# Unit-matrix products in the first cross-attention's last tiles and in TensorE's pauses at the heads and ends of the stages

## What is computed

```python
x = x + L0_xattn(ln(x), ctx, ctx, ...)      # 16 heads of 8, keys: 77 context tokens
x = x + L0_ffn(ln(x), ...)                  # 8 experts, relu, top 2, hidden 512
x = x + L1_xattn(ctx, ln(x), ...)           # latent attention: 16 heads of 64, keys: 77 context tokens and the 512 latents
x = x + L1_ffn(ln(x), ...)                  # 8 experts, swiglu, sampled number of experts
x = x + L2_xattn(ctx, ctx, ln(x), mask)     # 16 heads of 8, additive mask
x = x + L2_ffn(ln(x), ...)                  # mixture of 12, gelu, routed twice
x = x + L3_xattn(ln(x), ctx, mask)          # 8 heads of 64
x = x + L3_ffn(ln(x), ...)                  # 1 shared and 8 routed experts, gelu
```

```python
h = act(einsum('nd,df->nf', normed, W1[e]) + b1[e])
y = y + cw[:, e:e+1] * (h @ W2[e] + b2[e])
```

## Time and profile before

| | |
|---|---|
| median of 3 runs | 1892.74 us (1891.47 to 1894.18) |
| the profiled execution's own time | 1898.05 us |
| its span | 1896.2 us |
| TensorE busy | 1769.7 us (93%), weight loads 1304.8 us (69%) |
| VectorE, ScalarE, POOL busy | 77%, 55%, 37% |
| mean granted clock of TensorE | 0.966 |
| chain that ended last, by engine | PE 5%, DVE 1% of the span |

### The profile page before, as it was taken

The page is one execution under the profiler, slowest core; times in us unless marked ns, Lnnn a source line. Parts: engine busy times, 40 slices in busy tenths (PEclk is TensorE's granted clock), DMA queues, the critical chain, the costliest instruction groups (busy, mean ns, idle before and its releaser), DMA issues. The chain is left out here.

```text
span 1896.2 us, 29215 instructions
## 1 busy us (share of the span) xinstructions
PE 1769.7 (93%) x10747; PEld 1304.8 (69%) x10747; DVE 1461.0 (77%) x2712; ACT 1037.0 (55%) x1570; POOL 707.2 (37%) x571
## 2 busy tenths in 40 slices
PE   5998999779999999999989999799899999989898
PEld 4767888555655655655557777677658889957676
DVE  6877997767677777777767888799799955667798
ACT  3656888557777777777654555355200310055685
POOL 3632322145556556556430444455112301012131
PEclk9988999889999999999988999899899999999899
DMA  2001221100000000000001211000000010000032
GB/s 68 2 7 50 83 68 56 53 1 1 1 1 1 1 1 1 1 1 1 1 20 57 67 67 56 13 2 1 18 22 22 28 56 1 0 13 2 30 112 100
DMA packets 21191, 51.46 MB, mean 27 GB/s; under 512 B 3563, under 2 KB 11383, under 8 KB 18116
## 3 DMA queue, kind: packets, MB, share of 16 engines
q1 hardware_dynamic: 20596, 49.53, 7.7%
q10 hardware_dynamic: 464, 0.20, 0.1%
HBM read 48.48 MB, written 1.25 MB: 26 GB/s over the span
## 5 line engine op out<-in xcount | busy, mean ns | idle before, releaser
L1615 POOL TENSOR_TENSOR sb_L_total<-sb_L_total,sb_L_probT 128x512 f32<-128x512 f32 x128 | 161.4, 1293 | 170.4 <-ACT sb_L_probT L1953 170.4
L441 POOL TENSOR_TENSOR sb_L_prob<-sb_L_prob,sb_L_rsum 128x616 f32<-128x616 f32 (+1 forms) x96 | 105.7, 1123 | 227.9 <-DVE sb_L_rsum L743 227.9
L2021 DVE TENSOR_REDUCE sb_L_tops<-banks 128x2 f32<-128x1024 f32 x128 | 156.4, 1223 | 23.8 <-PE banks L1729 22.5
L1953 ACT ACTIVATE sb_L_probT<-banks 128x1024 f32<-128x1024 f32 x128 | 124.8, 1025 | 74.5 <-PE banks L1763 74.0
L1776 PE MATMUL banks<-sb_L_probT,sb_L_v 128*64 128x512 f32 x512 | 129.0, 605 | 0.0
L2403 DVE SCALAR_TENSOR_TENSOR sb_L2f_hid<-banks,sb_L2f_weight,sb_L2f_hid 128x512 f32<-128x512 f32 x176 | 122.0, 744 | 3.0 <-PE banks L97 1.6
L1612 POOL TENSOR_TENSOR sb_L_total<-sb_L_probT 128x512 f32<-128x512 f32 x64 | 93.7, 1488 | 78.9 <-ACT sb_L_probT L1953 78.9
L2473 DVE SCALAR_TENSOR_TENSOR sb_resid<-banks,sb_L2f_weight,sb_resid 128x128 f32<-128x128 f32 x192 | 67.1, 351 | 62.5 <-PE banks L97 57.9
L1315 DVE TENSOR_TENSOR sb_L0f_hid_low<-sb_L0f_raw,sb_L0f_hid_high 128x1024 fp32r<-128x1024 f32 x64 | 88.5, 1398 | 31.9 <-ACT sb_L0f_hid_high L1271 31.6
L1252 ACT ACTIVATE sb_L1f_gate<-banks 112x512 f32<-112x512 f32 x96 | 57.5, 599 | 91.3 <-PE banks L97 90.8
L529 PE MATMUL banks<-sb_ident,sb_L_prob 128*77 128x128 f32 x640 | 97.9, 286 | 5.7 <-POOL sb_L_prob L441 5.4
(11 more groups left out here) (433 smaller groups left out, 5336.0 us busy)
## 6 DMA issues: line engine op xcount, KB each, us to landing
sb_L0f_wide<-spread_L0f SPq DMA_DIRECT2D x7, 1024.0 KB, 6.9
sb_L1f_wide<-spread_L1f SPq DMA_DIRECT2D x7, 1024.0 KB, 7.7
sb_L3f_wide<-spread_L3f SPq DMA_DIRECT2D x7, 1024.0 KB, 4.7
sb_fetched<-L2f_w SPq DMA_DIRECT2D x12, 256.0 KB, 2.6
sb_fetched<-L1f_gu SPq DMA_DIRECT2D x8, 336.0 KB, 3.3
sb_fetched<-L0f_w SPq DMA_DIRECT2D x8, 259.0 KB, 2.8
sb_fetched<-L0f_w SPq DMA_DIRECT2D x8, 256.0 KB, 3.2
sb_normT<-L2f_w SPq DMA_DIRECT2D x2, 768.0 KB, 4.1
```

Source lines behind the costliest of these rows:

```text
L441: pool.tensor_tensor(grid, grid, bcast(rsum[:, n % PROBS, half], [None, KEYS]), ALU.mult).then_inc(normed, 1)
L1615: pool.tensor_tensor(sums, sums, probT[:, k, h], ALU.add).then_inc(added[h], 1)
L1953: act.activation(probT[:, k], ps[:, slot:slot + 2, :], ACT.Exp).then_inc(exped, 1)
L2021: dve.tensor_reduce(tops[:, :, k, 0], ps[:, banks:banks + 2, :], AX.X, ALU.max).then_inc(bound_read, 1)
```

## The change

It adds `keep_busy` in seven places of the code, and ahead of two of them a wait. In the order of the program: 8 products ahead of the key projection of each cross-attention (three stages); 5 in each of L0's last three tiles, before the third group's product, behind a wait that the scores of tile 15 have been read (`wait_scores_read`), because bank 0 held them; after the router's matmuls 20 in L0f and 6 in L3f; 10 at the end of L0f and L1f, ahead of the turn of the next norm; in latent attention 12 ahead of the first projection, 4 between two sums of squares, and 8 ahead of the turn of the maxima, behind a wait that VectorE has read the fourth bound, which stood further down before.

```diff
--- before.py
+++ after.py
@@ -467,6 +467,7 @@
             @block.tensor
             def _(pe):
                 fetch.wait(pe, "w")
+                keep_busy(pe, c, 3 if split else 2, 8)
                 for j in range(FB):
                     pe.matmul(ps[:, K_AT[j], 0:BATCH * KEYS], wk[:, j * P:(j + 1) * P], c.ctxT[:].rearrange("p b k -> p (b k)"),
                               start=True, stop=True).then_inc(k_done, 1)
@@ -572,6 +573,9 @@
                             turn(n, g + 1)
                         if g == SCORES_AT and later(n, AHEAD):
                             scores(n + AHEAD)
+                        elif g == SCORES_AT and split and not on_pe:
+                            wait_scores_read(TILES - 1)
+                            keep_busy(pe, c, 0, 5)
                         product(n, g)
                         next_queries()
                     if SCORES_AT == GROUPS and later(n, AHEAD):
@@ -1216,6 +1220,8 @@
                         hidden(s, f)
                 norm.wait(pe)
                 route.tensor(pe)
+                if not gated:
+                    keep_busy(pe, c, YBANKS[0], 20 if folded else 6)
                 norm.wait_parts(pe)
                 for s in range(STEPS):
                     then = s + lag
@@ -1233,6 +1239,7 @@
                         turn_back(s - STEPS + BATCH - 1)
                 if nxt is not None:
                     pe.wait_ge(out_read, STEPS - 1)
+                    keep_busy(pe, c, YBANKS[(STEPS - 3) % len(YBANKS)], 10)
                     nxt.norm.turn(pe, 0, SIDE)
                     nxt.norm.turn(pe, 1, YBANKS[(STEPS - 2) % len(YBANKS)])
                 turn_back(BATCH - 1)
@@ -1778,6 +1785,7 @@
                             last = pe.matmul(O[HEAD[h]], vc[:, p % 2, b, HEAD[h]], probT[0:KEYS, k, h, :], start=False, stop=True)
                     last.then_inc(pv_done, 1)
 
+                keep_busy(pe, c, 0, 12)
                 use_side(KC, 0)
                 fetch.wait(pe, "values")
                 use_side(VC, 0)
@@ -1787,6 +1795,7 @@
                 use_side(NKC, 0)
                 use_side(NKL, 0)
                 wait_read(pe, KC, 0)
+                keep_busy(pe, c, 0, 4)
                 use_side(NQL, 0)
                 norm.wait_parts(pe, 1)
                 wait_read(pe, VC, 0)
@@ -1814,6 +1823,8 @@
                 bound(0, 3, 0)
                 bound(0, 4)
                 wait_read(pe, Q, 1)
+                pe.wait_ge(bound_read, 4)
+                keep_busy(pe, c, 0, 8)
                 use_side(MT, 0)
                 wait_read(pe, V4, 0)
                 wait_read(pe, NQL, 1)
```

## The result

The changed kernel takes **1905.39 us** (median of 6 runs, 1903.11 to 1909.06), the kernel before 1893.53 beside it (1891.47 to 1894.62). The ratio is 1.0065, 95% interval 1.0053 to 1.0077: **12.3 us slower** by the ratio (11.9 by the two medians), where the forecast was +1.1 and the range ended at 1901. In what follows, microseconds beside a ratio are its distance from 1 times 1893. A run of 4295.35 us of the kernel before and one of 2244.65 us of e12 are in none of the ratios. The profiled execution of the changed kernel took 1907.01.

What follows compares the result with a forecast made beforehand. TensorE running part of the time at half clock around stage changes was taken as the bound; the terms summed to +1.1 us, 1893.8 on the median (1899.1 on the profiled execution), range 1885 to 1901.

Steps and rivals of the forecast that it cites:

- Head of the first cross-attention: Eight products at half clock ahead of the key projection, a chain without slack, paid whole: +3.5 us.
- Its last tiles and the start of L0f: L0's last tiles keep the clock up, -2.7 us; L0f's old products then run at full clock, another -2.7.
- 20 products after the router: In L0f: mostly cold, overrunning the idle time by about 1.3 us, but saving 2.5 behind it: -1.2 us.
- L0f's end, latent attention's start: Ten products hidden in idle time; twelve overrun cold by 3.2 us, most given back by faster projections: +0.6 us.
- the first bound's turn: Latent attention's 8 products fill 1.7 us of idleness: -2.8 us at full clock, about +1.1 if it fell; taken -1.3.
- there nothing changes: Long middles of dense experts and latent attention stay as they are; a late start shifts the end by as much.
- L2's head: Eight cold products cost 3.5 us, less 0.6 for a faster key projection and some hidden by VectorE's moments: +2.0.
- L3's: Eight products at the head of L3, which TensorE starts at full clock, delay what hangs on it: +1.7 us.
- L3f: Six products after its router, where TensorE waits only 0.21 us, add 1.3 us of full-clock work: +1.2.
- third rival: Every clock fall comes where it came and only costs are left: 17.6 us, 1910; chance 0.05.
- The rule against the change: Transposes don't bring the clock to full, so five products a tile in L0 may be too few.
- The slower rival: Five products a tile are too few, or the clock falls at L0's end: 5.5 us more, 1899.3; chance 0.20.

Runs made afterwards that it cites:

- e12: Four products in place of eight at the head of the first cross-attention, nothing else, against the kernel before: 1.0027.
- e14: Eight products at the head of the first cross-attention alone, against the kernel before, a repeat of e6: 1.0025.
- e15: The same kernel as e6 and e14, compared once more with the kernel before: 1.0024.
- e6: Eight products at the head of the first cross-attention alone, against the kernel before: 1.0048.
- e16: The kernel before, unchanged, timed as if changed and profiled a second time: 1.0009; profiled execution 1891.35 us.
- e1: Only the five products in each of L0's last three tiles, against the kernel before: 1.0002.
- e3: Only the 20 products after L0f's router and the 6 after L3f's, against the kernel before: 1.0006.
- e9: Only the ten products at the ends of L0f and L1f, against the kernel before: 1.0006.
- e4: Only latent attention's 12, 4 and 8 products and the wait that moved up, against the kernel before: 1.0011.
- e10: The kernel before with five unit products as a plain delay in turn 3 of latent attention's dense loop: 1.0008.
- e7: Eight products at the head of L2's cross-attention alone, against the kernel before: 1.0031.
- e8: Eight products at the head of L3 alone, against the kernel before: 1.0014.
- e2: Only the eight products ahead of the key projection in all three cross-attentions, against the kernel before: 1.0058.
- e17: The changed kernel plus eight unit products in latent attention's last pause, against the kernel before: 1.0057.
- e5: The whole change without the eight products at the three heads, against the kernel before: 1.0039.
- e18: The changed kernel without the heads' and routers' products, plus eight in latent attention's last pause, against the kernel before: 0.9993.

## Why the prediction was wrong, by its steps

*Head of the first cross-attention, +3.5.* Right, by the mechanism given: 4.0 in the profile. The median cost is a little more, +4.5 to +4.7 us in e14 and e15, with e6 higher.

*Its last tiles and the start of L0f, -2.7 and -2.7.* **This step failed.** Against the first profile both came: 139.88 to 141.44 is +1.6 behind a +4.0, so -2.4, and VectorE's second split of L0f's head went from 154.47 to 153.23, -2.8 more. But I put the sum on the median, as if the fall at 128.6 came in every execution. The profiled one lay 5.3 us over the median, and against e16's profile these are the falls themselves: 3.4 us at L0f's first products and 6.2 at its loop. 11 of 14 profiles without tile products don't have the long fall, and there the tiles cost 1.1 and win nothing. e1 measured +0.4 where the two terms sum to -5.4. The forecast even wrote "if it usually falls a tile earlier", and never "if it usually doesn't fall".

*20 products after the router, -1.2.* Wrong sign in this profile: from -1.2 at VectorE's split to +3.2 at the loop's first product (164.70 to 167.89), and 0.5 behind at L0f's last sum, +1.7. The forecast had 4.6 us of idleness left for them, with TensorE done with the router 1.8 earlier; it was done at 160.95, 1.7 later than before, and VectorE's split ended at 163.40, so 2.45 were left for products that ran 6.9. Alone (e3) +1.1, not told from nothing.

*L0f's end, latent attention's start and the first bound's turn, +0.6 and -1.3.* The profile has +0.4 for both together (355.73 to 356.21, then 412.04 to 412.91); e9 and e4 can't be told from nothing.

*Not in the forecast: latent attention's end, +2.4.* I had written that "there nothing changes" of the long middles. At the end of this one stands a pause in which the clock can fall, and it fell where the products in latent attention's head, or e10's delay, had made the distance from the clock's last rise longer.

*L2's head, +2.0, and L3's, +1.7.* Mis-sized: 3.4 and 2.6 (from 6.7 to 9.3 behind the first profile); e7 has +5.9 and e8 +2.7 us. In L2 I took 1.5 off the 3.5 us, 0.6 for a faster key projection and the rest hidden by VectorE's moments. In the changed kernel's profile nothing came off between the key projection and the scores reduction; in those of e2, e7 and e17 0.6 to 1.2 did. In L3 the eight cost their full-clock time, 1.9, and 0.8 more by L3's softmax. *L3f, +1.2:* -0.3.

*The bound's turn, a slip.* The 8 products at half clock take 3.5 us where 1.7 are idle, which is 1.8 over; the +1.1 given for that end isn't worked out in the text. It changes an end of that term and the third rival's sum, not the forecast.

The sum of these for the two first profiles is 4.0 - 2.4 - 2.8 + 1.7 + 0.4 + 2.4 + 3.4 + 2.6 - 0.3 = 9.0, the spans' difference. What the medians have beyond that is the luck of the profile of before, 4.5 us over its median, less the 1.6 of the changed one: 9.0 + 4.5 - 1.6 = 11.9. The heads are the cause that the runs show best: +11.0 us by themselves, but only 4.9 come back when they are taken out of the changed kernel (12.3 against e5's 7.4), so their share of the 12.3 stays uncertain by that much. In the table they are 3.9 + 3.4 + 1.9 + 0.8 = 10.0 of 16. The rest is nothing that can be told once the heads and the routers' products are gone and the pause is filled (e18). That 11.0 and 7.4 sum to 6.1 more than 12.3 is just outside the 5 or so that their intervals together allow.

None of the three rivals names this cause. The third, in which only costs are left, has the heads, the router's 20 and the tiles nearer to what was measured than the others have, and latent attention too high; but it gives another reason: it lets every fall come where it came, and in most executions the fall that the change was to remove isn't there.

**The rule against the change.** The slower rival went by the clock falling among transposes in spite of five products. What the profiles show is another thing: of 14 profiles of these tiles without any product, 9 kept the clock at 1.00 throughout them. The Trainium skill (TensorE: Matmul & The Clock Gate, Part 4: PE-mode transpose), which says that transposes don't count as busy in the same way, agrees with the long falls (0.50 from 128.6 on, while the transposes ran, in the first profile of before) and doesn't tell the two kinds of execution apart.

## What to carry over

Products that keep the clock up belong only where the engine waits longer than they take, counted at the clock that is granted *there*: eight in the last pause of latent attention, reached at full clock, took 2.05 us of a 2.77 us wait, while the 20 behind L0f's router took 6.9 where 2.45 were left. Ahead of the first instruction of a chain without slack they are paid whole, at the low clock, and no later gain returned them here (eight at three heads: +11 us). Before a gain is read off a cold stretch in a profile, compare that execution's time with the median: what it has in excess is missing from most runs, and a second profile of the same kernel shows which stretch it is. For effects under half a per cent on such a kernel, one comparison of six runs is not enough: the same kernel gave 1.0048 and 1.0024.

## What the runs showed of the hardware

Executions of the unchanged kernel spread from 1888.97 to 1901.61 us over 118 runs (e16's own eight reach 1902.64), and its two profiles show one source of it: some 129 us of the span recorded at half clock in the one and 105 in the other, and the difference at L0's end and in L0f makes 6.5 us (355.73 against 349.19). The Trainium skill (TensorE: Matmul & The Clock Gate, Part 1: The HAM clock gate) says that the gate's rhythm runs on freely and isn't reset when a kernel starts; two executions of one program with different falls agree with that. It also puts the ramp penalty, for modelling, at under 1% of a typical kernel span and advises against fitting a specific count of cold matmuls; here two executions differ by 0.35%, so a forecast to 0.2% can't be read from one of them.

A later pause is tied to the clock's last rise: over 530 us of unbroken work the distance varied by under 2 us in 20 profiles, and in the 17 with an empty pause 0.4 us of it divided those whose clock held from those whose clock fell.
